# Rotary attention: both masks added by TensorE, GpSimd left with the head products, VectorE with plain maxima

## Chip, cores and metric

The kernel runs on one core of a Trainium2 chip. The metric is the device time of one execution in microseconds (us), lower is better. It is a chain of eight layers over 16 sequences of 512 tokens with 128 features, taken in pairs of sequences. The change touches one layer only, the third attention (rotary, causal, softmax).

## What is computed

The layer in question, cut to what matters. `x` is (16, 512, 128), there are 16 heads of 8 features. `_rope` with `d_param` = 128 multiplies each row by a table (the halves are never swapped, since `mid` is larger than the head).

```python
q = _rope(proj(Wq, bq), e)
k = _rope(proj(Wk, bk), e)
v = proj(Wv, bv)
att = jnp.einsum('bhqd,bhkd->bhqk', q, k) / scale
causal = jnp.tril(jnp.ones((t, t), dtype=bool))
att = jnp.where(causal[None, None], att, -jnp.inf)
att = jax.nn.softmax(att, axis=-1)
y = jnp.einsum('bhqk,bhkd->bhqd', att, v)
```

## The kernel before, in words

The program has three parts (`PARTS`), each a loop over the eight pairs of sequences, with an expert stage between the first and the second. The rotary attention is the first layer of the second part, so it runs eight times. Each loop body is written engine by engine; engines wait for one another by semaphores only, and each works through its own list in order.

**Quartets and steps.** The 16 heads of a sequence are four quartets, so a pair has eight (`QUARTETS`), numbered c. The four heads of a quartet lie in the four groups of 32 partitions. Work on a quartet is cut into six steps u. A step takes two heads and one set of tiles: the query tiles 3, 2, or 1 and 0 (`TILES_OF`), or the key tiles 0, 1, or 2 and 3 (`KEYS_OF`). So a step is 512, 384, or 256+128 columns wide for each of its two heads, and each width occurs in two steps.

**Two kinds of scores.** `scores(c, u)` makes row scores (queries on partitions), of which only the maximum of each row is wanted. `scores_t(c, u)` makes transposed scores (keys on partitions), of which the exponent is taken and which then weigh the values. The maxima are turned (`turn_max`) and added to the queries (`shift`), so that the transposed scores come out shifted. TensorE's list, for c from -2 to 8 and u from 0 to 5, is

```python
scores_t(c, u)
scores(c + 2, u)
```

with `values` (u = 0, 1, 4), `turn_max(c + 1)` (u = 1) and `spread_sums(c - 1)` (u = 3) behind them. All eight quartets thus pass in ten and a half rounds: two with row scores alone (c = -2, -1), six with both kinds (c = 0 to 5), two with transposed scores alone (c = 6, 7) and a rest. The two heads of `scores_t(c, u)` are `2 * (1 - u % 2) + e`, those of `scores(c + 2, u)` are `2 * (u % 2) + e`: the other two row groups of the array.

**Buffers.** Both kinds write three double banks of PSUM (`twin[n % 3]`) in turn (`SLOTS`). So `scores_t(c, u)` waits for the maxima of step u-2 (signal `l2_max`), and `scores(c + 2, u)` for the exponents of `scores_t(c, u - 1)` (`l2_exp`).

**Masks.** VectorE's `maxima` (line 792) is one `tensor_tensor_reduce` for each head and tile: it adds `mask_row` (zeros, then a triangle of -1e30) and takes the negated maximum, by a custom instruction and a read of its accumulator. The exponents are not masked; GpSimd's `mask` (lines 597 and 601) sets the blocks on the diagonal to zero with `affine_select` afterwards and raises `l2_masked`, for which `values` waits.

**Other work beside it.** A previous pair's last layer (attention over heads) is spread over this stage: GpSimd's `product` (line 651, 16 of them, two before the masks and 14 among them in `l2_masks`) and VectorE's `take` (lines 1364 and 1367), at fixed steps (`TAKE_STEP`). A product waits for the take two before it (`f_read`), a take for its product (`f_pool`). GpSimd's list in `l2_masks` is the masks of steps 0 and 1, a product, the masks of steps 2 to 5, a product, and so on for seven quartets.

**Names and lines.** TensorE: `scores` 1761, `scores_t` 1779, `values` 1802 (in `weigh`), `turn_max` 1848, `spread_sums` 1861, each of which a profile shows by its line; every fp32 matmul appears as two instructions in it. ScalarE: exponents 1435, `take_values` 1445, `invert` 1454 and 1456. VectorE: `divide` 808, `shift` 816.

Of the kernel before, what the change touches and what calls it, by code (L numbers as in the profile page):

```python
# [54 lines left out]
def program(nc, dram, x_in, out, sorted_x, sorted_y, kept_x, routes, returns, starts):  # L55
    with ExitStack() as ctx:
# [268 lines left out]
        for first, last in PARTS:  # L325
# [214 lines left out]
            with nc.Fori(0, SEQS // 2 if first < LAYERS else 1) as pair:  # L540
                sg = Signals()
                with nc.Block(no_gpsimd_drain=True) as block:
# [44 lines left out]
                    def _(pool):  # L587
                        def mask(tag, c, u):
# [4 lines left out]
                            p = at_pt[tag][n % len(at_pt[tag])]  # L593
                            pool.wait_ge(sg[tag + "_exp"], n + 1)
                            if u < 4:
                                p = p[:, :, 0:P]
                                pool.affine_select(p, p, [[0, 2], [1, P]], ALU.is_ge, 0.0, base=0,  # L597
                                                   channel_multiplier=-1).then_inc(sg[tag + "_masked"], 1)
                            else:
                                p = p.rearrange("p e (b k) -> p e b k", b=2)[:, :, :, 0:P]  # L600
                                pool.affine_select(p, p, [[0, 2], [0, 2], [1, P]], ALU.is_ge, 0.0, base=0,
                                                   channel_multiplier=-1).then_inc(sg[tag + "_masked"], 1)

                        def l1_masks():
# [22 lines left out]
                            for c in range(-2, QUARTETS + 1):  # L627
                                split(c + 1)
                                for u in range(STEPS_OF):
                                    mask("l1", c, u)  # L630
                                    if 0 <= c < QUARTETS and u % 3 == 1:
                                        send_rows(pool, sg, (2 * QUARTETS + 2 * c + u // 3,))
# [50 lines left out]
                        for layer in range(first, min(last, LAYERS)):  # L683
# [30 lines left out]
                            if layer == L2_ATTENTION:  # L714
# [3 lines left out]
                                l2_masks()  # L718
# [13 lines left out]
                    def _(dve):  # L732
# [43 lines left out]
                        def twin_attention(tag, beside):  # L776


                            def maxima(c, u):
# [5 lines left out]
                                for e in range(2):  # L785
                                    j = 2 * (u % 2) + e
                                    at = 0
                                    for i in TILES_OF[u // 2]:
                                        w = P * (i + 1)
                                        into = at_nmax[c % 4][:, i, j:j + 1] if tag == "l1" else at_shift[c % 2][  # L790
                                            :, i, j, DH:DH + 1]
                                        last = dve.tensor_tensor_reduce(  # L792
                                            s[:, e, at:at + w], s[:, e, at:at + w], W["mask_row"][:, T - w:T], -1.0, 3e38,
                                            ALU.add, ALU.min, into)
                                        at += w
                                last.then_inc(sg[tag + "_max"], 1)
# [903 lines left out]
                    def _(pe):  # L1700
# [23 lines left out]
                        def twin_attention(tag, row_sets, of_value, beside):  # L1724
# [16 lines left out]
                            def scores(c, u):  # L1741
# [801 lines left out]
```

## Time and profile before

| | us |
|---|---|
| median of 3 runs | 6046.7 (6040.18 to 6059.04) |
| profiled execution, first to last instruction (its span) | 6032.4 |
| PE busy / DVE busy / ACT busy / POOL busy | 4713.6 / 3697.0 / 1851.2 / 2161.3 |

The profiled execution shows its span; its own time is that and what lies around it, and the median of the runs is 14.3 us above the span. PE is TensorE's matmuls, PEld its weight loads, DVE VectorE, ACT ScalarE, POOL GpSimd. PE's busy time is to be read with care: matmuls overlap and their ends are modelled, so starts say more than durations. PEclk is the granted clock as a share of 2.4 GHz; it takes the values 1.0 and 0.5 (1.2 GHz), and anything between is a mean over a stretch.

The rotary attention of a pair is found by its first row scores and by the first instruction of the projection that follows it: 3595.5 and 3733.2 us for the third pair, and 136 to 140 us for each of the eight.

### The profile page before, as it was taken

The page shows a single profiled execution, that of the slowest core. Times are in us where ns is not written, and L with a number is a line of the kernel's source. Part 1 is how long each engine was busy: PE and PEld are TensorE (multiplying, and loading weights), DVE is VectorE, ACT ScalarE, POOL GpSimd, SP SyncE. Part 2 cuts the span into 40 slices and gives each one's busy share as a digit, 9 for nine tenths or more (in the row PEclk, how much of TensorE's full clock was granted, in tenths as well). Part 3 has the DMA queues.
Part 4 walks back from the last instruction along what each step waited for, and adds up shares of the span by engine and source line. Part 5 has one row for each costly group of instructions (what it writes and reads, how often), then busy time and mean ns, then how long its engine had stood idle before and what let it go on. Part 6 is the DMA issues. An engine that isn't in the chain of part 4 may idle for free. (4 is left out here: it accounts for less than half of the span.)

```text
span 6032.4 us, 97232 instructions
## 1 busy us (share of the span) xinstructions
PE 4713.6 (78%) x37160; PEld 2735.5 (45%) x37160; DVE 3697.0 (61%) x11081; ACT 1851.2 (31%) x2829; POOL 2161.3 (36%) x2704
## 2 busy tenths in 40 slices
PE   5979797979797979595877868778687786877772
PEld 3444445444444444363443544535435444354442
DVE  3646464646464646364768567686686766857765
ACT  2333343334333334242323224132331322412320
POOL 1323232323232222444525236153361443614525
PEclk9989898989898989797888888888888888888886
DMA  4000000000000000372000000000000000000000
GB/s 146 6 18 6 18 6 18 6 18 6 18 6 18 6 18 6 112 232 74 4 15 13 8 20 4 15 14 6 18 6 12 18 5 17 8 9 20 3 15 5
DMA packets 141914, 146.71 MB, mean 24 GB/s; under 512 B 31256, under 2 KB 126042, under 8 KB 141042
## 3 DMA queue, kind: packets, MB, share of 16 engines
q1 hardware_dynamic: 114274, 93.48, 5.3%
q0 software_dynamic: 18432, 37.79, 2.2%
q10 hardware_dynamic: 8736, 8.91, 0.5%
q8 instruction: 326, 5.34, 0.4%
q14 instruction: 146, 1.20, 0.1%
HBM read 69.64 MB, written 62.59 MB: 22 GB/s over the span
## 5 line engine op out<-in xcount | busy, mean ns | idle before, releaser
L792 DVE CUSTOM_DVE_ANT_0 twin<-twin,w_mask_row 128x512 f32<-128x512 f32 (+3 forms) x2048 | 951.0, 521 | 329.7 <-PE twin L1761 328.3
L1761 PE MATMUL twin<-arena 32*128 32x128 f32 (+3 forms) x4096 | 799.4, 517 | 39.6 <-DMA arena<-hres 16.8
L1779 PE MATMUL twin<-arena 32*128 32x128 f32 (+3 forms) x4096 | 784.2, 499 | 35.3 <-DVE arena L792 33.9
L1707 PE MATMUL twin<-w_ident_b 128*128 128x512 bf16 x1536 | 454.9, 450 | 383.7 <-DVE mv L752 157.9
L1435 ACT ACTIVATE arena<-twin 128x768 f32<-128x768 f32 (+1 forms) x544 | 479.3, 881 | 691.6 <-PE twin L1790 387.5
L1779 PEld LDWEIGHTS twin<-arena 32*128 32x128 f32 x4096 | 342.8, 195 | 471.7 <-issue 283.3
L695 POOL TENSOR_SCALAR ve<-mv 128x4 f32<-128x4 f32 x128 | 27.7, 216 | 1467.8 <-DVE mv L752 1467.2
L321 POOL DMA_INDIRECT got<-sorted_y,back x288 | 281.1, 976 | 539.6 <-ACT ring L1641 289.0
L1707 PEld LDWEIGHTS twin<-w_ident_b 128*128 128x128 bf16 x1536 | 157.7, 112 | 651.5 <-DVE mv L752 180.6
L313 POOL DMA_INDIRECT sorted_x<-got,w_mo_first_slots x288 | 282.4, 981 | 467.5 <-DVE ring L866 302.2
L1761 PEld LDWEIGHTS twin<-arena 32*128 32x128 f32 x4096 | 353.6, 204 | 196.8 <-issue 109.2
L1802 PE MATMUL twin<-arena 128*32 128x128 f32 (+3 forms) x2944 | 305.8, 459 | 18.6 <-POOL arena L597 18.6
L792 DVE DVE_READ_ACCUMULATOR2_ANT arena<- 128x1 f32 x2048 | 292.4, 143 | 0.0
L597 POOL TENSOR_SCALAR_AFFINE_SELECT arena<-arena 128x256 f32<-128x256 f32 x352 | 143.0, 409 | 342.7 <-ACT arena L1435 342.5
L1435 ACT ACTIVATE ring<-twin 128x768 f32<-128x768 f32 (+1 forms) x224 | 194.0, 878 | 198.6 <-PE twin L1779 197.6
L701 POOL TENSOR_TENSOR rs<-ve,minus_half 128x4 f32<-128x4 f32 x208 | 223.6, 1075 | 17.3
L2180 PE MATMUL twin<-w_l3f_we,arena 128*128 128x128 f32 x1152 | 191.1, 320 | 47.7 <-DVE arena L1115 47.7
L651 POOL TENSOR_TENSOR w_mo_wgu<-w_mo_wgu,w_l_cs_feat 128x2048 f32<-128x2048 f32 x36 | 197.3, 5483 | 54.5 <-DVE w_mo_wgu L1364 27.7
L1802 PE MATMUL twin<-ring,arena 128*32 128x384 f32 (+3 forms) x1152 | 155.7, 497 | 64.1 <-POOL ring L597 57.5
L651 POOL TENSOR_TENSOR w_mo_wgu<-w_mo_wgu 128x2048 f32<-128x2048 f32 x36 | 200.3, 5568 | 13.5 <-DVE w_l_wo L1367 13.5
L2180 PEld LDWEIGHTS twin<-w_l3f_we,arena 128*128 128x128 f32 x1152 | 163.9, 221 | 88.9 <-DVE arena L1115 63.6
L1364 DVE TENSOR_REDUCE w_mo_wgu<-w_mo_wgu 128x128 f32<-128x1024 f32 x144 | 174.6, 1217 | 22.6 <-POOL w_mo_wgu L651 22.6
(440 smaller groups left out, 10008.1 us busy)
## 6 DMA issues: line engine op xcount, KB each, us to landing
sorted_y<-arena SPq DMA_DIRECT2D x96, 256.0 KB, 2.8
sorted_x<-zeros ACTq DMA_DIRECT2D x2, 4096.0 KB, 19.9
a<-sorted_x SPq DMA_DIRECT2D x64, 128.0 KB
b<-sorted_x SPq DMA_DIRECT2D x64, 128.0 KB, 2.5
hres<-sorted_x SPq DMA_DIRECT2D x64, 128.0 KB
sorted_x<-got,w_mo_first_slots POOLq DMA_INDIRECT x288
got<-sorted_y,back POOLq DMA_INDIRECT x288
x_out<-w_l_w SPq DMA_DIRECT2D x18, 256.0 KB, 2.3
```

The costliest lines, as they stand in the source:

```text
L313: pool.indirect_dma_start(sorted_x[r % GROUPS], bass.IndirectOffsetOnAxis(ap=slot_of[:, q, n:n + 1], axis=0), normed[q][:, r // GROUPS], N ...
L321: pool.indirect_dma_start(got[q][:, n], None, sorted_y, bass.IndirectOffsetOnAxis(ap=back[:, q, n:n + 1].bitcast(U32), axis=0)).then_inc(s ...
L651: pool.tensor_tensor(pr, left.broadcast_to(shape), right.broadcast_to(shape), ALU.mult).then_inc(sg["f_pool"], 1)
L701: pool.tensor_tensor(RS[q][:], VE[q][:], minus_half[:], ALU.pow).then_inc(sg["rstd_ready"], 1)
L792: last = dve.tensor_tensor_reduce(s[:, e, at:at + w], s[:, e, at:at + w], W["mask_row"][:, T - w:T], -1.0, 3e38, ALU.add, ALU.min, into)
L1364: i = dve.tensor_reduce(ht_sc[q][:, t, heads], ht_pr[m % 2].rearrange("p (h g d) -> p h g d", h=H, g=H)[:, heads], AX, ALU.add)
L1435: act.activation(at_pt[tag][n % len(at_pt[tag])][:, :, 0:w], twin[SLOT["scores_t", c, u] % 3][:, :, 0:w], ACT.Exp, scale=1.0 if tag == "l1 ...
L1707: pe.matmul(into, ident_b, ident_b.unsqueeze(1).broadcast_to([P, NT, P]), start=True, stop=True, skip_group_check=True)
L1761: last = pe.matmul(s[:, e, at:at + w], queries[r, P * i:P * (i + 1)], keys[r, 0:w], start=(at == 0), stop=True, skip_group_check=True)
L1779: last = pe.matmul(s[:, e, at:at + w], keys[r, P * m:P * (m + 1)], queries[r, P * m:T], start=(at == 0), stop=(tag == "l2"), skip_group_ch ...
L1802: last = pe.matmul(bank[into][rows_of(j), P * m:T], weights(m, j), at_pt[tag][n % len(at_pt[tag])][:, j % 2, at:at + w], start=(m == 0), s ...
L2180: i = pe.matmul(pb3(q, 3)[:, t], mo_fb[q][:, (e - 1) % 2, t * P:(t + 1) * P], weights[:, (e - 1) * P:e * P], start=(e == 1 and t == 0), st ...
```

## The change

In the rotary attention (tag `l2`) only:

- `scores` adds, behind the score matmuls of each step, one bf16 matmul for each of the two heads: identity times the triangle of `mask_row`, onto the diagonal blocks (128 columns, or 256 in the steps with two tiles). VectorE's `maxima` becomes one plain `tensor_reduce` over both heads for each tile.
- `scores_t` adds the same with `mask_tb` on its diagonal blocks, so that the exponents come out masked. GpSimd's masks go, and `values` waits for `l2_exp` instead of `l2_masked`.
- GpSimd's list is then the 14 products one behind another.

```diff
-                        def l2_masks():
-                            for c in range(QUARTETS):
-                                for u in range(STEPS_OF):
-                                    mask("l2", c, u)
-                                    if u == 1 and c < HEAD_QUARTETS:
-                                        product(2 + 2 * c)
-                                if c < HEAD_QUARTETS:
-                                    product(3 + 2 * c)
+                        def head_products():
+                            for m in range(2, 4 * NT):
+                                product(m)
...
+                                j = 2 * (u % 2)
+                                if tag == "l2":
                                     at = 0
                                     for i in TILES_OF[u // 2]:
                                         w = P * (i + 1)
-                                        into = at_nmax[c % 4][:, i, j:j + 1] if tag == "l1" else at_shift[c % 2][
-                                            :, i, j, DH:DH + 1]
+                                        last = dve.tensor_reduce(at_shift[c % 2][:, i, j:j + 2, DH], s[:, :, at:at + w], AX,
+                                                                 ALU.max, negate=True)
+                                        at += w
+                                    last.then_inc(sg["l2_max"], 1)
+                                    return
...
                                     for e in range(2):
                                         r = rows_of(2 * (u % 2) + e)
                                         last = pe.matmul(s[:, e, at:at + w], queries[r, P * i:P * (i + 1)], keys[r, 0:w],
-                                                         start=(at == 0), stop=True, skip_group_check=True)
+                                                         start=(at == 0), stop=(tag == "l1"), skip_group_check=True)
                                     at += w
+                                if tag == "l2":
+                                    diagonal = slice(P * TILES_OF[u // 2][0], P * TILES_OF[u // 2][0] + P * len(TILES_OF[u // 2]))
+                                    masks = W["mask_row"][:, T - P:T].unsqueeze(1).broadcast_to([P, len(TILES_OF[u // 2]), P])
+                                    for e in range(2):
+                                        last = pe.matmul(s[:, e, diagonal], ident_b, masks, start=False, stop=True,
+                                                         skip_group_check=True)
                                 last.then_inc(sg[tag + "_scores"], 1)
...
+                                if tag == "l2":
+                                    for e in range(2):
+                                        blocks = s[:, e].rearrange("p (b k) -> p b k", b=2)[:, 0:len(KEYS_OF[u // 2]), 0:P]
+                                        masks = W["mask_tb"].unsqueeze(1).broadcast_to([P, len(KEYS_OF[u // 2]), P])
+                                        last = pe.matmul(blocks, ident_b, masks, start=False, stop=True, skip_group_check=True)
...
-                                pe.wait_ge(sg[tag + "_masked"], STEPS_OF * c + 2 * b + 2)
+                                pe.wait_ge(sg["l1_masked" if tag == "l1" else "l2_exp"], STEPS_OF * c + 2 * b + 2)
```

TensorE's list in a round with both kinds, steps 1 and 2, before (1779 transposed scores, 1761 row scores, 1848 `turn_max`, 1802 `values`):

```order
L1779 MATMUL twin<-arena 128x512 x2
L1761 MATMUL twin<-arena 128x512 x2
L1848 MATMUL twin<-w_ident,arena 128x128 x4
L1802 MATMUL twin<-arena 32x256 x4
L1802 MATMUL twin<-arena 32x128 x4
L1779 MATMUL twin<-arena 128x384 x2
L1761 MATMUL twin<-arena 128x384 x2
```

and the same steps now (1787, 1763, 1861 and 1815 are those lines moved; 1794 and 1770 are the masks):

```order
L1787 MATMUL twin<-arena 128x512 x2
L1794 MATMUL twin<-w_mask_tb,w_ident_b 128x128 x2
L1763 MATMUL twin<-arena 128x512 x2
L1770 MATMUL twin<-w_mask_row,w_ident_b 128x128 x2
L1861 MATMUL twin<-w_ident,arena 128x128 x4
L1815 MATMUL twin<-arena 32x256 x4
L1815 MATMUL twin<-arena 32x128 x4
L1787 MATMUL twin<-arena 128x384 x2
L1794 MATMUL twin<-w_mask_tb,w_ident_b 128x128 x2
L1763 MATMUL twin<-arena 128x384 x2
L1770 MATMUL twin<-w_mask_row,w_ident_b 128x128 x2
```

Where transposed and row scores stood next to each other, a pair of masks now stands between them and another behind them.

GpSimd's list from the first products on, before (651 products, 597 and 601 masks):

```order
L651 TENSOR_TENSOR w_mo_wgu<-w_l_wo,w_l_cs_feat 128x2048 x2
L597 AFFINE_SELECT arena<-arena 128x2x128 x2
L651 TENSOR_TENSOR w_mo_wgu<-w_l_wo,w_l_cs_feat 128x2048
L597 AFFINE_SELECT ring<-ring 128x2x128 x2
L601 AFFINE_SELECT ring<-ring 128x4x128
L601 AFFINE_SELECT arena<-arena 128x4x128
L651 TENSOR_TENSOR w_mo_wgu<-w_l_wo,w_l_cs_feat 128x2048
```

and all of it now:

```order
L651 TENSOR_TENSOR w_mo_wgu<-w_l_wo,w_l_cs_feat 128x2048 x4
L651 TENSOR_TENSOR w_mo_wgu<-absorbed_q,w_mo_wgu 128x2048 x4
L651 TENSOR_TENSOR w_mo_wgu<-w_mo_wgu,w_l_cs_feat 128x2048 x4
L651 TENSOR_TENSOR w_mo_wgu<-w_mo_wgu 128x2048 x4
```

The 16 products keep their order; the 48 masks of a pair are gone from between them.

## Rows read from the trace of the kernel before

**Rows 1.** The page: its span.
```profile
span 6032.4 us, 97232 instructions
```

**Rows 2.** Windows of one pair: stretch, length, busy PE, PEld, DVE, ACT, POOL, clock
```profile
3595.50:3611.70 16.20, 14.07 (x70) 7.90 (x70) 14.91 (x52) 0.00 (x0) 7.71 (x2) 0.58 0.13 25
3611.70:3703.00 91.30, 75.31 (x600) 31.32 (x600) 86.67 (x251) 42.82 (x54) 71.60 (x48) 0.89 0.03 7
3703.00:3733.20 30.20, 23.47 (x154) 8.79 (x150) 11.81 (x14) 14.23 (x20) 22.27 (x15) 0.76 0.00 1
```

**Rows 3.** Windows, one round of the first pair, same columns.
```profile
2847.50:2858.20 10.70, 10.54 (x108) 4.81 (x100) 9.15 (x35) 5.60 (x7) 10.70 (x7) 1.00 0.13 25
```

**Rows 4.** Timeline of PE in one round: start us, duration, instruction, count
```profile
3649.40 1.06 PE L1802 MATMUL twin<-ring,arena 128*32 128x512 f32 x8
3650.40 0.48 PE L1779 MATMUL twin<-arena 32*128 32x256 f32 x2
...
3651.18 1.07 PE L1779 MATMUL twin<-arena 32*128 32x512 f32 x4
3652.32 1.13 PE L1761 MATMUL twin<-arena 32*128 32x512 f32 x4
3653.38 0.52 PE L1802 MATMUL twin<-arena 128*32 128x384 f32 x2
...
3654.16 0.70 PE L1779 MATMUL twin<-arena 32*128 32x512 f32 x2
3654.18 0.70 PE L1761 MATMUL twin<-arena 32*128 32x512 f32 x2
...
3654.71 0.59 PE L1761 MATMUL twin<-arena 32*128 32x512 f32 x2
3655.23 0.66 PE L1848 MATMUL twin<-w_ident,arena 128*128 128x128 f32 x4
3655.82 0.41 PE L1802 MATMUL twin<-ring,arena 128*32 128x256 f32 x2
...
3656.61 0.59 PE L1779 MATMUL twin<-arena 32*128 32x384 f32 x2
...
3657.04 0.49 PE L1779 MATMUL twin<-arena 32*128 32x384 f32 x2
...
3661.18 1.10 PE L1861 MATMUL twin<-hres,w_sel_sum 128*128 128x512 f32 x2 [1.50 <-issue]
3662.20 0.48 PE L1779 MATMUL twin<-arena 32*128 32x256 f32 x2
```

**Rows 5.** Timeline of PE in another layer: a 512-column bf16 identity times mask.
```profile
3105.57 0.63 PE L2247 MATMUL twin<-w_mask_tb,w_ident_b 128*128 128x512 bf16 x1
3106.00 0.63 PE L2255 MATMUL twin<-arena 128*128 128x128 f32 x2
```

**Rows 6.** Groups by line, 3645.1 to 3660.4: count | busy, mean ns | idle before
```profile
L792 DVE CUSTOM_DVE_ANT_0 twin<-twin,w_mask_row 128x384 f32<-128x384 f32 (+3 forms) x16 | 7.4, 518 | 0.6 <-PE twin L1761 0.6
...
L1364 DVE TENSOR_REDUCE w_mo_wgu<-w_mo_wgu 128x128 f32<-128x1024 f32 x4 | 4.9, 1216 | 0.0
```

**Rows 7.** Timeline of DVE, two maxima by their widths.
```profile
3654.90 0.69 DVE L792 CUSTOM_DVE_ANT_0 twin<-twin,w_mask_row 128x512 f32<-128x512 f32 x1
...
3649.60 0.43 DVE L792 CUSTOM_DVE_ANT_0 twin<-twin,w_mask_row 128x256 f32<-128x256 f32 x1 [0.61 <-PE twin L1761]
```

**Rows 8.** Groups by line, 2600 to 5900 us: slowest products, matmuls that weigh values.
```profile
L651 POOL TENSOR_TENSOR w_mo_wgu<-w_mo_wgu 128x2048 f32<-128x2048 f32 x32 | 178.5, 5579 | 13.5 <-DVE w_l_wo L1367 13.5
...
L1802 PE MATMUL twin<-ring,arena 128*32 128x384 f32 (+3 forms) x1152 | 155.7, 497 | 64.1 <-POOL ring L597 57.5 <-POOL ring L601 6.1
...
L1802 PE MATMUL twin<-arena 128*32 128x256 f32 (+3 forms) x896 | 128.6, 500 | 18.6 <-POOL arena L597 18.6
```

**Rows 9.** Windows, a dense stretch of the same pair, columns as in rows 2.
```profile
3622.00:3640.00 18.00, 17.75 (x154) 7.21 (x146) 16.63 (x59) 9.64 (x13) 16.05 (x14) 1.00 0.08 16
```

**Rows 10.** Timeline at the pair's end: ScalarE takes the last values.
```profile
3729.46 0.60 ACT L1445 ACTIVATE arena<-twin 128x512 f32<-128x512 f32 x1 [1.69 <-PE twin L1802]
```

More of the change, by code:

```diff
@@ L587, in _, with mask @@
                     def _(pool):
-                        def mask(tag, c, u):
+                        def mask(c, u):
                             if not 0 <= c < QUARTETS:
@@ L592, in mask @@
                             n = STEPS_OF * c + u
[L593 to L594 removed]
+                            p = at_pt["l1"][n % len(at_pt["l1"])]
+                            pool.wait_ge(sg["l1_exp"], n + 1)
                             if u < 4:
@@ L629, in l1_masks @@
                                 for u in range(STEPS_OF):
-                                    mask("l1", c, u)
+                                    mask(c, u)
                                     if 0 <= c < QUARTETS and u % 3 == 1:
@@ L784, in maxima @@
                                 s = twin[SLOT["scores", c, u] % 3]
-                                for e in range(2):
-                                    j = 2 * (u % 2) + e
+                                j = 2 * (u % 2)
+                                if tag == "l2":
                                     at = 0
@@ L789, in maxima @@
                                         w = P * (i + 1)
-                                        into = at_nmax[c % 4][:, i, j:j + 1] if tag == "l1" else at_shift[c % 2][
-                                            :, i, j, DH:DH + 1]
+                                        last = dve.tensor_reduce(at_shift[c % 2][:, i, j:j + 2, DH], s[:, :, at:at + w], AX,
[4 more added lines that the diff above has]
+                                for e in range(2):
+                                    at = 0
+                                    for i in TILES_OF[u // 2]:
+                                        w = P * (i + 1)
                                         last = dve.tensor_tensor_reduce(
                                             s[:, e, at:at + w], s[:, e, at:at + w], W["mask_row"][:, T - w:T], -1.0, 3e38,
-                                            ALU.add, ALU.min, into)
+                                            ALU.add, ALU.min, at_nmax[c % 4][:, i, j + e:j + e + 1])
                                         at += w
-                                last.then_inc(sg[tag + "_max"], 1)
+                                last.then_inc(sg["l1_max"], 1)
                             def divide(c):
@@ L1779, in scores_t @@
                                         last = pe.matmul(s[:, e, at:at + w], keys[r, P * m:P * (m + 1)], queries[r, P * m:T],
-                                                         start=(at == 0), stop=(tag == "l2"), skip_group_check=True)
+                                                         start=(at == 0), stop=False, skip_group_check=True)
                                     at += w
+                                if tag == "l2":
+                                    for e in range(2):
+                                        blocks = s[:, e].rearrange("p (b k) -> p b k", b=2)[:, 0:len(KEYS_OF[u // 2]), 0:P]
+                                        masks = W["mask_tb"].unsqueeze(1).broadcast_to([P, len(KEYS_OF[u // 2]), P])
+                                        last = pe.matmul(blocks, ident_b, masks, start=False, stop=True, skip_group_check=True)
                                 if tag == "l1":
```

6 lines of the change are left out of this document (3 added, 3 removed).

## Prediction

> **What bounds the kernel now.** The page gives the span, 6032.4 us [rows 1]; the median of the runs is 14.3 us above it, and I carry that difference along. The change touches one stage that runs eight times, so the windows come next, cut where its kinds of round change [rows 2]. A pair's rotary attention is 16.2 + 91.3 + 30.2 = 137.7 us, eight of them some 1100 us of the span. In the middle stretch (six rounds with both kinds of scores, 15.2 us each) DVE is busy 86.67 of 91.3 us, 95%, and POOL 71.6. PE's 75.3 is 82%, at a granted clock of 0.89. So DVE bounds the middle, with the maxima and the takes in its list. In the tail DVE is busy 11.8 of 30.2 us: there PE waits for masks that stand in POOL's list behind products of up to 5.58 us [rows 8]. The groups by line show that wait: matmuls of `values` found PE idle for 64.1 + 18.6 = 82.7 us over the eight pairs, and nearly all of it ended by a mask [rows 8].
>
> The margin of PE matters most, and the busy column hides it. It has to be read from starts in PE's timeline [rows 4]. The transposed scores of a 512 step alone start at 3651.18, the row scores of the next at 3652.32 and what follows at 3653.38: 1.14 and 1.06 us apart, each for two heads. At 3654.16 and 3654.18 both kinds start together, on the four different row groups, and the next instruction starts at 3655.23: 1.07 us for **four** heads. The second kind costs nothing where it stands next to the first. That is what keeps PE below DVE. The round of the first pair at 2847.5, before the takes weigh on DVE, shows PE's floor: 10.54 busy of 10.70 us at clock 1.00 [rows 3].
>
> **PE in a round, now.** From starts [rows 4]: a 512 step costs 1.07 us; a 384 step twice the distance 3656.61 to 3657.04, 0.86; a 256+128 step 3650.40 to 3651.18, 0.78. Two of each are 5.42. `values` is 1.00 (3649.40 to 3650.40), 0.78 (3653.38 to 3654.16) and 0.79 (3655.82 to 3656.61), 2.57 together; `turn_max` 0.59; `spread_sums` 1.02 (3661.18 to 3662.20). With both kinds overlapping in five steps of six (step 0 is apart, +1.07) that makes 5.42 + 1.07 + 2.57 + 0.59 + 1.02 = 10.67, which is the 10.70 of [rows 3].
>
> **What the masks do to it.** A mask is an identity matmul over all 128 rows. PE takes its matmuls in order, so the masks of `scores_t` wait until its two row groups have streamed, and `scores` on the other two groups waits for the masks. None of the six steps can overlap any more: the two kinds cost 2 x 5.42 = 10.84. The masks themselves are 12 pairs in a round, eight of 128 and four of 256 columns. Streaming alone: 512 bf16 columns took 0.43 us at half clock (3105.57 to 3106.00) [rows 5], so 0.055 per 128 at full clock, 8 x 0.11 + 4 x 0.22 = 1.8 us. That is the low bound. For the high bound I take `turn_max`, whose four transposes cost 0.59 with both handovers, 0.15 each: 8 x 0.30 + 4 x 0.41 = 4.0. I take 3.0, since of the two rows the transposes are the nearer for the handovers and the bf16 row for the streaming. A round with both kinds is then 10.84 + 3.0 + 2.57 + 0.59 + 1.02 = **18.0 us of PE**, against 15.2 us that it takes today. PE becomes the bound.
>
> In the trace the full-array transpose starts 0.52 us after the last pass over 32 rows (3654.71 to 3655.23), as far as one pass lies behind the other (3654.18 to 3654.71) [rows 4]: the switch costs nothing extra there, and the sum has no term for it. The Trainium skill (TensorEngine Tiling (Array Packing), Tiling Modes) says that changing the tiling mode, not just the tile, drains the engine. By that rule each of a round's 24 switches would cost extra; the trace does not agree, by that 0.52, and it is among the rivals below.
>
> **DVE and POOL.** The maxima of a round are 16 custom instructions, 7.4 us busy [rows 6]. Width costs 0.26 us per 256 elements, on top of 0.17 (0.69 at 512, 0.43 at 256) [rows 7], and a 1024-wide reduce, from SBUF, takes 1.22 [rows 6], on the same line. Eight reduces of 1024, 768, 512, 256 (twice) are 5120 elements and eight fixed parts: 5.2 + 1.4 = 6.6, so 0.8 us less, and the accumulator reads go too. Taking both, DVE needs some 14.2 us where it had 15.2. That is below 18.0 and no longer on the path. Its reduces are done in time: PE needs the maxima of step u-2 for `scores_t(u)`, and at least 2 us of other PE work now lie between. The 48 selects removed from POOL are worth nothing in the middle (cover: PE's own 18 us); in the tail they end PE's waits. The 14 moved products wait only for takes. Two products take at most 11.2 us [rows 8] of an 18 us round, so they are early, and in the tail the last three end some 17 us after its start, inside PE's 27. No DMA moves, SP's list stays as it is, and ScalarE's exponents are the same. `values` now waits for the exponents alone, which are two or more steps old. The edit of `stop` in the earlier attention changes no instruction count; I cost it at nothing.
>
> **The sum for a pair.** Middle: six rounds of 18.0 = 108.0 against 91.3, +16.7. Start (16.2 us now): twelve row-score groups, 10.84, twelve pairs of masks, 3.0, and a `turn_max`, 0.59, are 14.4 at full clock. The mean clock there is 0.58, mostly the lower level of 1.2 GHz, after PE has waited for the rotated rows and with DVE setting its pace [rows 2]; it is 1.00 where PE is packed, 17.75 of 18 us [rows 9]. PE will now be packed from the start; I allow 6 us at half clock, costing 3: 17.4, +1.2. Bounds: 14.4 (-1.8) and all at half clock, 28.8 (+12.6). Tail (30.2 now): round 6 is 5.42 + 1.5 + 2.57 + 0.59 + 1.02 = 11.1, round 7 10.5, the last two `values` 1.6 and the chain from there to the end 3.8 (3729.46 to 3733.2) [rows 10]: 27.0, -3.2. Waits at handovers, 0.16 a round as in [rows 3]: +1.3. Together +16.0 a pair, x 8 = **+128 us**: 6046.7 + 128 = 6175.
>
> **Rivals.**
> - *DVE stays the bound, faster.* If the masks only queue between scores that go on overlapping, PE needs 10.7 + 3.0 = 13.7 a round, below DVE's 14.2. Then six rounds give -6, the start -2, and the tail loses its mask waits, -6: -14 a pair, 5935. It decides where PE's round falls below 14.2. For it: the handover to the transpose is free, and nothing in the trace shows a full-array matmul between two row groups that could overlap. Against it: in rows 4 no full-array instruction starts before the row groups have had their whole pass, and the masks stand between the kinds in every step. 0.12.
> - *Nothing to measure.* Masks at their low bound (16.8 a round) and a fast start and tail leave +3 a pair; it would need 1 us more of luck. With a partial overlap the sum crosses zero: 6047. 0.05.
> - *Drains.* If each switch waits for the pipeline to empty, its price is the 0.16 by which a 384 pass (0.59) outlasts the 0.43 to the pass behind it [rows 4]; 24 switches are 3.8 us a round, and over the eight quartets 31 a pair: +47, 6423. Against it: the 0.52 above. 0.07.
> - *The change isn't what it says.* PE's and POOL's lists show it is: masks between the kinds, products in one row. No chance is kept for it.
>
> **How the numbers follow.** The forecast has 0.76. Its own range: low, masks 1.8 (six rounds 100.8, +9.5), start -2.4, tail -4.2: +3 a pair, 6070. High, masks 4.0 (19.0 a round, +22.7), start +14.6, tail -1: +36, 6337. A measurement of this kernel can tell about 0.3%, 18 us, from no change. The faster rival lies outside the range and so does the drain; of the forecast's own spread the range keeps nearly all: 6075 to 6335. Faster 0.12, same 0.05, slower 0.76 + 0.07 = 0.83.
>
> **What would show it.** In the profile after: rounds in the middle of 17 to 19 us; PE's starts of 1763 always behind a mask, never within 0.02 us of 1787; a granted clock near 1.0 in the middle; DVE down from 95% to below 80% there; no wait of 1815 for POOL; about 108 us for the middle and 27 for the tail. Wrong it is if starts of 1763 still fall together with those of 1787's two heads, if a mask pair costs over 0.4 us, or if the half clock lasts through the start.

## The result: 7% slower, and the profile after

The changed kernel takes 6484.3 us, median of 4 runs (6468.4 to 6541.8); the kernel before, run beside it, 6043.4 (6028.9 to 6059.0). The ratio is 1.074, with a 95% interval of 1.070 to 1.078. The forecast was 6175, its range 6075 to 6335, so the sign and the bound are right, and the size is off by 309 us, outside the range. Medians and ratios here leave out executions in a slower state, of which there were two: 6604.0 us in the run with key masks alone, and 8213.6 us of the kernel before. In the changed kernel's lines `scores` is 1763, `scores_t` 1787, the row masks 1770, the key masks 1794, `values` 1815, `turn_max` 1861 and the maxima 785.

The span on the page of after; and, from the groups by line of 2600 to 6200 us, the two groups of `values`, with the idle time before them in the last column:
```profile
span 6479.0 us, 98384 instructions
```
```profile
L1815 PE MATMUL twin<-ring,arena 128*32 128x384 f32 (+3 forms) x1152 | 175.2, 552 | 0.2
...
L1815 PE MATMUL twin<-arena 128*32 128x256 f32 (+3 forms) x896 | 142.3, 544 | 0.0
```
`values` found PE idle for 82.7 us before [rows 8]; now it is 0.2 us. `values` no longer waits for POOL's masks. That part did what it was to do.

Windows over whole pairs, from the first row scores to the output projection. First the kernel after, its third, fifth and sixth pair and the sum of all eight; columns as in [rows 2]:
```profile
...
3701.20:3884.10 182.90, 177.88 (x1009) 73.71 (x1009) 109.21 (x123) 58.19 (x74) 78.33 (x16) 0.79 0.03 6
...
4580.80:4785.40 204.60, 199.63 (x1008) 80.55 (x1008) 109.37 (x123) 58.21 (x74) 78.29 (x16) 0.70 0.03 5
5034.70:5216.20 181.50, 176.50 (x1009) 73.42 (x1009) 109.15 (x123) 58.18 (x74) 78.30 (x16) 0.80 0.03 6
...
sum 1543.50, PE 1503.19 PEld 614.79 DVE 873.94 ACT 465.57 POOL 625.63; mean PE 187.90 PEld 76.85 DVE 109.24 ACT 58.20 POOL 78.20
```
The same for the kernel before, its third pair and the sum of all eight:
```profile
3595.50:3733.20 137.70, 112.85 (x816) 48.01 (x816) 113.40 (x315) 57.06 (x74) 101.58 (x64) 0.83 0.04 7
...
sum 1097.60, PE 903.09 PEld 384.36 DVE 908.68 ACT 456.82 POOL 807.65; mean PE 112.89 PEld 48.05 DVE 113.59 ACT 57.10 POOL 100.96
```
The stage grew by 1543.5 - 1097.6 = 445.9 us and the span by 446.6: all of the loss is here. PE is busy 97% of the stage, DVE 57%. And the pairs, which run the same instructions, differ by 23 us, with the granted clock: 0.70 in the slowest, 0.80 in the fastest. The clock is what has to be read next.

Windows of the slowest pair, round by round:
```profile
4580.80:4604.70 23.90, 23.87 (x94) 10.43 (x94) 15.46 (x18) 0.00 (x0) 11.53 (x3) 0.56 0.14 26
4604.70:4632.90 28.20, 28.20 (x103) 11.26 (x102) 8.23 (x11) 5.29 (x6) 5.17 (x2) 0.50 0.06 11
4632.90:4665.80 32.90, 32.90 (x129) 12.58 (x128) 10.38 (x12) 7.05 (x9) 4.49 (x1) 0.50 0.00 0
4665.80:4690.00 24.20, 24.20 (x128) 9.52 (x130) 14.47 (x17) 7.98 (x10) 8.99 (x2) 0.72 0.00 1
4690.00:4708.00 18.00, 18.00 (x128) 7.88 (x130) 13.62 (x17) 7.03 (x9) 9.96 (x2) 1.00 0.00 1
...
4743.90:4785.40 41.50, 36.55 (x187) 13.21 (x186) 19.47 (x19) 15.86 (x21) 16.29 (x3) 0.67 0.00 0
```
PE is busy without a gap from the start of the pair on, and still has the lower clock, 1.2 GHz, for the start and two rounds and a half. Then the clock rises to 2.4 GHz, and a round with the same 128 matmuls takes 18.00 us instead of 32.90. The mean falls again in the tail, to 0.67. The other seven pairs do the same over shorter stretches: their six rounds take 116 to 131 us, and in all eight the last three rounds are 18.0 us at 1.00. In the kernel before, the half clock of the third pair ended within the first round, and the second ran at 1.00:
```profile
3611.70:3623.70 12.00, 11.62 (x77) 5.26 (x77) 11.20 (x43) 4.39 (x5) 5.72 (x5) 0.72 0.13 24
3623.70:3635.60 11.90, 11.71 (x108) 5.04 (x106) 10.68 (x36) 6.90 (x10) 9.95 (x7) 1.00 0.11 20
```

The timeline of PE at 1.00 shows what a step has become:
```profile
2904.78 1.13 PE L1787 MATMUL twin<-arena 32*128 32x512 f32 x4
2905.84 0.28 PE L1794 MATMUL twin<-w_mask_tb,w_ident_b 128*128 128x128 bf16 x2
2906.06 1.13 PE L1763 MATMUL twin<-arena 32*128 32x512 f32 x4
2907.12 0.28 PE L1770 MATMUL twin<-w_mask_row,w_ident_b 128*128 128x128 bf16 x2
2907.33 0.85 PE L1815 MATMUL twin<-ring,arena 128*32 128x384 f32 x8
...
2910.45 0.28 PE L1770 MATMUL twin<-w_mask_row,w_ident_b 128*128 128x128 bf16 x2
2910.57 0.61 PE L1861 MATMUL twin<-w_ident,arena 128*128 128x128 f32 x4
```
Each kind has its own 1.06 us now, where both shared 1.07 before [rows 4], and a pair of masks costs 0.21 to 0.22 with both switches. Ahead of another full-array product, the transposes of `turn_max`, it costs 0.12 (2910.45 to 2910.57). So there are two losses: the order of the round, and the clock in which it runs.

### The profile page after: what moved, and what is told of

Same layout as the page of the kernel before. It is cut to its first block and busy times, and to the rows that moved or that the text cites. A ratio compares the mean times of both kernels' runs of the same rounds, so it can differ in the third digit from the quotient of the medians.

```text
span 6479.0 us, 98384 instructions
## 1 busy us (share of the span) xinstructions
PE 5309.6 (82%) x38696; PEld 2964.1 (46%) x38696; DVE 3666.7 (57%) x9545; ACT 1859.5 (29%) x2829; POOL 1976.2 (31%) x2320
## 5 line engine op out<-in xcount | busy, mean ns | idle before, releaser
L1763 PE MATMUL twin<-arena 32*128 32x512 f32 (+3 forms) x4096 | 877.0, 534 | 20.5 <-DMA arena<-hres 16.8
L1787 PE MATMUL twin<-arena 32*128 32x512 f32 (+3 forms) x4096 | 867.0, 525 | 1.3
L785 DVE TENSOR_REDUCE arena<-twin 128x2 f32<-128x1024 f32 (+3 forms) x512 | 409.8, 822 | 502.3 <-PE twin L1770 502.1
L794 DVE CUSTOM_DVE_ANT_0 twin<-twin,w_mask_row 128x512 f32<-128x512 f32 (+3 forms) x1024 | 478.6, 520 | 274.0 <-PE twin L1763 273.0
L1787 PEld LDWEIGHTS twin<-arena 32*128 32x128 f32 x4096 | 370.2, 207 | 453.8 <-issue 303.5
L1763 PEld LDWEIGHTS twin<-arena 32*128 32x128 f32 x4096 | 370.8, 210 | 178.4 <-issue 126.7
L1815 PE MATMUL twin<-arena 128*32 128x128 f32 (+3 forms) x2944 | 319.6, 472 | 0.0
L651 POOL TENSOR_TENSOR w_mo_wgu<-absorbed_q,w_mo_wgu 128x2048 f32<-128x2048 f32 x36 | 162.1, 4507 | 399.0 <-DVE w_mo_wgu L1366 399.0
L651 POOL TENSOR_TENSOR w_mo_wgu<-w_l_wo,w_l_cs_feat 128x2048 f32<-128x2048 f32 x36 | 160.7, 4477 | 229.8 <-DVE w_mo_wgu L1366 156.9
```

The costliest lines, as they stand in the source:

```text
L651: pool.tensor_tensor(pr, left.broadcast_to(shape), right.broadcast_to(shape), ALU.mult).then_inc(sg["f_pool"], 1)
L785: last = dve.tensor_reduce(at_shift[c % 2][:, i, j:j + 2, DH], s[:, :, at:at + w], AX, ALU.max, negate=True)
L794: last = dve.tensor_tensor_reduce(s[:, e, at:at + w], s[:, e, at:at + w], W["mask_row"][:, T - w:T], -1.0, 3e38, ALU.add, ALU.min, at_nmax ...
L1787: last = pe.matmul(s[:, e, at:at + w], keys[r, P * m:P * (m + 1)], queries[r, P * m:T], start=(at == 0), stop=False, skip_group_check=True)
L1815: last = pe.matmul(bank[into][rows_of(j), P * m:T], weights(m, j), at_pt[tag][n % len(at_pt[tag])][:, j % 2, at:at + w], start=(m == 0), s ...
```

## The experiments

Two theories stood against each other. A: the masks between the kinds end their overlap; this costs PE its margin, and PE's unmerged passes over 32 rows leave the clock at 1.2 GHz, however busy it is. B: the mask products themselves hold the clock down, or cost more than they show. The clock after a dense burst, the overlap and the masks are varied one at a time. Each ratio is to the kernel before, run on the same chip; before had medians of 6023 to 6040 us there.

**Only the key masks on PE.** DVE's masked maxima as before.
```diff
-for e in range(2):
-    last = pe.matmul(s[:, e, diagonal], ident_b, masks, start=False, stop=True,
-                     skip_group_check=True)
...
-last = dve.tensor_reduce(at_shift[c % 2][:, i, j:j + 2, DH], s[:, :, at:at + w], AX,
-                         ALU.max, negate=True)
+last = dve.tensor_tensor_reduce(
+    s[:, e, at:at + w], s[:, e, at:at + w], W["mask_row"][:, T - w:T], -1.0, 3e38,
+    ALU.add, ALU.min, into)
```


> The changed kernel with DVE's old masked maxima: only the masks of the transposed scores are on PE. They stand between the transposed group and the group of scores of the same step, so they break one of the two meetings. Theory A: with one break left PE's round at full clock is 15.5 to 16.5 us, the half clock lasts into the rounds but shorter than in the changed kernel: 6200 to 6400 us. Rival B (each mask costs the same, wherever it is): halfway, 6200 to 6320. Rival D (DVE's plain maxima are what cost time): under 6100 us.

6528.9 us (6504.9 to 6599.9), ratio 1.083 (1.077 to 1.089): no faster than with both masks (1.070 to 1.078), and outside what any of the three theories gave. Windows of one pair (its six rounds), then one round at each clock:
```profile
5075.20:5251.30 176.10, 176.07 (x658) 70.12 (x660) 84.43 (x239) 42.45 (x53) 52.85 (x11) 0.50 0.02 3
```
```profile
5100.00:5130.30 30.30, 30.30 (x118) 11.89 (x116) 11.59 (x36) 7.05 (x9) 4.47 (x1) 0.50 0.00 1
3783.00:3799.30 16.30, 16.30 (x115) 7.22 (x114) 14.62 (x41) 7.04 (x9) 9.51 (x3) 1.00 0.00 1
```
At full clock this round is 1.7 us shorter than 18.0, as a round should be that has no overlap either and six pairs of masks fewer (10.84 for the scores, 4.2 for the rest and some 1.4 for six pairs). The only meeting that overlapped before is the one between the two kinds of the same step: `scores(c + 2, u)` and the next `scores_t(c, u + 1)` have the same two row groups. So key masks alone end all of the overlap, not half of it, as the expectation had it. The run lost because it left the half clock late or never: in three pairs the six rounds took 176 us, with PE busy for 176.07 of 176.10 in the pair shown; in the other five they took 112 to 169. The Trainium skill (TensorE: Matmul & The Clock Gate, The HAM clock gate) says that activity releases the throttle and that a busy PE runs warm. By that rule these six rounds would have taken some 98 us, six times 16.3; the trace does not agree, and the measurement decides.

**The overlap reduced without any mask on PE.** The kernel before, with the transposed scores on the row groups of their neighbour.
```diff
-r = rows_of(2 * (1 - u % 2) + e)         # scores_t
+r = rows_of(2 * ((1 - u % 2) if tag == "l1" else u % 2) + e)
...
-n = STEPS_OF * c + 2 * b + 1 - j // 2    # weigh: the buffer of a head's exponents
+n = STEPS_OF * c + 2 * b + (1 - j // 2 if tag == "l1" else j // 2)
```


> The kernel before with one line's worth of difference: the transposed scores of a step use the same two row groups as its scores, so that the first of the two meetings of a step no longer runs side by side. No mask is on PE. It breaks the meeting that the run with key masks alone broke (6564 us there, with half clock for up to 176 us a pair). Theory A (loss of the overlap, not the mask products, keeps the clock down): PE's round at full clock is 14.5 to 15.2 us, half clock lasts into the rounds of most pairs, time 6200 to 6550 us. Rival B (the mask products keep it down): clock as before, round near 15, time 6030 to 6110 us.

6214.9 us (6186.4 to 6226.6), ratio 1.029 (1.024 to 1.034). One pair, start, six rounds and tail; then one round of another pair:
```profile
4051.30:4067.50 16.20, 14.09 (x70) 7.92 (x70) 14.95 (x52) 0.00 (x0) 7.67 (x2) 0.55 0.13 25
4067.50:4175.90 108.40, 101.69 (x582) 46.47 (x584) 83.12 (x239) 40.93 (x52) 67.06 (x43) 0.74 0.03 6
4175.90:4212.00 36.10, 26.73 (x173) 9.88 (x169) 21.40 (x26) 16.25 (x22) 26.62 (x20) 0.76 0.00 0
```
```profile
3676.80:3700.50 23.70, 23.70 (x107) 10.44 (x106) 11.50 (x36) 7.05 (x9) 11.66 (x8) 0.50 0.01 2
```
The six rounds grow from 86 to 108 us and their clock falls from 0.90 to 0.74, with no mask on PE; the round of the last line is packed and stays at 0.50. So less overlap is enough to lower the clock, which speaks for A.

Here the clock went in and out, and in the run before it stayed down much longer. The two do not lose the same: with this edit, the scores of a step and the transposed scores of the next lie on different row groups, and there they run side by side. The timeline shows it (1761 is `scores`, 1779 the next step's `scores_t`):
```profile
3676.81 0.64 PE L1761 MATMUL twin<-arena 32*128 32x256 f32 x2
3676.82 1.22 PE L1779 MATMUL twin<-arena 32*128 32x512 f32 x2
```
The overlap has moved and shrunk, not gone: a packed round at half clock takes 23.7 us here and 30.3 with the key masks, of which their six pairs are some 2.4 (0.32 us each at 128 columns, 0.54 at 256). What is still open is why the key masks alone kept the clock down longer than both masks did.

**A dense burst ahead of the start, or ahead of the rounds.** The changed kernel, and 18 bf16 products of 512 columns from its own `keep_busy`, once before the row scores of a pair, once before the first round with both kinds.
```diff
 pe.wait_ge(sg["l2_v"], 2)
+keep_busy(bank[6], *[(None, 0)] * 3)     # ahead of the start
```
```diff
 for c in range(-2, QUARTETS + 1):
+    if (tag, c) == ("l2", 0):            # ahead of the rounds
+        keep_busy(bank[6], *[(None, 0)] * 3)
```


> The changed kernel with 18 plain bf16 products of 512 columns on PE ahead of each pair's rotary stage, which the kernel uses elsewhere to keep PE busy. Theory A, first form (the clock needs dense full-array work to rise, and once up stays up in the masked mix): the burst costs 4 to 8 us a pair, the start and the first rounds then run at 18 us and under instead of 26 us and over, 20 to 50 us a pair less: 6150 to 6350 us. Second form (the masked mix itself draws the clock down at the start, whatever came before it): half clock in the start and the first rounds again, time 6480 to 6560 us.

> The changed kernel with the burst of 18 dense bf16 products of 512 columns moved from ahead of the start to ahead of the first round with both kinds. In the run with the burst ahead of the start the start ran at full clock in 15.6 us and the clock fell again in the first round. If the masked, unmerged rounds can hold the full clock once they have it (they do late in every pair), all rounds are 18.0 us: middle 108 us against 116 to 139, burst 5 to 8 us, time 6310 to 6400 us. If the clock falls in the first rounds whatever came before, 6450 to 6560 us.

The first: 6405.7 us, ratio 1.064 (1.058 to 1.070), between the two forms that I had written down. The start gained, 15.6 us in all eight pairs; the rounds did not, 115 to 153 us. One pair, start and rounds, and the beginning of the rounds of another:
```profile
3243.80:3259.40 15.60, 14.64 (x93) 6.86 (x92) 13.44 (x16) 0.00 (x0) 5.86 (x3) 1.00 0.14 25
3259.40:3412.60 153.20, 153.17 (x730) 61.36 (x730) 76.46 (x89) 42.39 (x53) 53.30 (x11) 0.65 0.02 4
```
```profile
2826.60:2854.00 27.40, 27.36 (x98) 11.02 (x98) 9.99 (x13) 5.29 (x6) 8.08 (x2) 0.50 0.09 16
```
The second: 6288.9 us, ratio 1.044 (1.038 to 1.050), some 190 us below the changed kernel for one burst a pair, and a little below the range written down. One pair, start with burst, rounds, tail:
```profile
4494.80:4524.00 29.20, 29.18 (x110) 12.61 (x110) 16.57 (x20) 0.00 (x0) 12.21 (x3) 0.59 0.14 26
4524.00:4629.40 105.40, 105.40 (x731) 46.33 (x730) 73.06 (x84) 42.36 (x53) 49.84 (x10) 1.00 0.01 2
4629.40:4661.80 32.40, 27.31 (x188) 10.53 (x186) 19.60 (x19) 15.74 (x21) 16.33 (x3) 0.89 0.00 1
```
The instructions of these rounds are those of the changed kernel. There they took 116 to 139 us; lifted once, they hold 1.00 to the end and take 105.4 in all eight pairs. So the mask products do not hold the clock down (against B), and at full clock PE's rounds cost what the sum said. The row scores of the start leave PE at 1.2 GHz, and unmerged rounds climb out of it late. The level at which the rounds begin does not settle it alone: behind the burst ahead of the start they began at 1.00 too, and the clock fell in the first round. Behind a burst directly ahead, the same first round, without `values` in both runs, held 1.00 and took 15.5 us. What in the start makes that difference is open.

**The overlap restored.** The changed kernel, both kinds next to each other and both groups of masks behind them.
```diff
 scores_t(c, u)
 scores(c + 2, u)
+if tag == "l2":
+    mask_keys(c, u)                      # was inside scores_t
+    mask_rows(c + 2, u)                  # was inside scores
```


> The changed kernel, with the two score groups of a step again next to each other and both groups of mask products behind them. Theory A (what the change lost is the overlap of the two kinds of scores, and while it is lost the granted clock stays near 0.5): the groups share PE again, so a round at full clock costs PE 5.7 (scores) + 2.2 to 3.0 (masks) + 2.57 + 0.59 + 1.02 = 12 to 13 us, DVE's 12.5 or so becomes the bound, the clock rises after the start of a pair as in the kernel before, and the time is 5930 to 6080 us. Rival B (the masks' full-array products themselves hold the clock down or cost far more than 0.22 to 0.33 us a pair): the half clock stays for 50 to 95 us a pair as in the changed kernel, time over 6250 us.

6078.5 us (6048.1 to 6114.6), ratio 1.009 (1.005 to 1.013): some 400 us below the changed kernel with the same instructions, only reordered. PE in one step and its masks (in this kernel 1794 is `scores_t`, 1763 `scores`, 1819 the key masks, 1777 the row masks), then one whole pair, then one round at full clock:
```profile
2861.04 0.49 PE L1794 MATMUL twin<-arena 32*128 32x384 f32 x2
2861.06 0.49 PE L1763 MATMUL twin<-arena 32*128 32x384 f32 x2
2861.48 0.29 PE L1819 MATMUL twin<-w_mask_tb,w_ident_b 128*128 128x128 bf16 x2
2861.60 0.28 PE L1777 MATMUL twin<-w_mask_row,w_ident_b 128*128 128x128 bf16 x2
2861.80 0.59 PE L1794 MATMUL twin<-arena 32*128 32x384 f32 x2
```
```profile
3601.70:3625.60 23.90, 23.90 (x92) 10.34 (x92) 15.43 (x18) 0.00 (x0) 11.41 (x3) 0.56 0.14 25
3625.60:3709.80 84.20, 83.67 (x731) 39.48 (x730) 73.89 (x87) 41.50 (x53) 48.34 (x11) 0.98 0.02 5
3709.80:3751.30 41.50, 36.56 (x188) 13.19 (x186) 19.46 (x19) 16.61 (x22) 18.65 (x4) 0.67 0.00 0
```
```profile
2866.47:2880.36 13.89, 13.89 (x127) 6.54 (x126) 13.66 (x17) 7.29 (x11) 9.30 (x3) 1.00 0.00 1
```
The kinds start together again (2861.04 and 2861.06), the half clock ends within the first round, in this pair and in the others, and the six rounds take 84.2 us (84 to 89 over the eight pairs), where they took 86 before (86 to 89). PE is still the bound of them, 99% busy: the expectation that DVE would be it was off by a little (DVE is at 88%, and at 13.66 of 13.89 us in the full round). What is left of the loss is in the start (24 to 26 us, 16 before) and in the tail (31 to 43, before 33 to 36), where only one kind exists and the masks still part the groups.

**Parts of it.** Three smaller runs. Row masks on PE alone, key masks on POOL; then the same with the row masks issued only where an overlap ends anyway; then plain maxima with no row mask at all (that part is left out).
```diff
 scores(c + 2, u)
+if tag == "l2":                          # second run: row masks placed
+    if c + 2 < QUARTETS:
+        unmasked.append((c + 2, u))
+    if u % 2 if c < 0 else u not in (2, 5):
+        while unmasked:
+            mask_rows(*unmasked.pop(0))
```


> The kernel before, with row masks alone on PE, behind the group of scores, and plain maxima on DVE; the masks of the transposed scores stay products of Pool. A row mask now stands behind each second group, so half of the meetings of the two kinds are left. Theory A: PE's round is 1 to 1.5 us longer than before and stays at or under 14.4 us, DVE is 0.8 to 1.1 us shorter, time 5990 to 6100 us. Rival B (masks hold the clock): half clock well into the pair's rounds, time over 6150 us. Rival C (Pool's products were the bound of the tail): tails unchanged at 33 to 36 us, since Pool's work is unchanged.

> The kernel before with row masks on PE and plain maxima on DVE as in the run with row masks alone (6073 us), but the row masks are issued only where the groups' overlap ends anyway: in the start behind every second group, in the rounds ahead of the value, turn and sum products, never between the scores of one step and the transposed scores of the next. Key masks stay on Pool. Theory A: the start falls from 24 to 16 us a pair, the rounds lose the broken meetings: 5980 to 6020 us, at or under the kernel before. Rival (the maxima that come a step later delay the slots or the shift): 6040 us and more.

> The kernel before with plain maxima of two heads on DVE in the rotary stage and no mask of the row scores at all (that part of the computation is left out: the maxima are taken over unmasked scores, which changes the shift of the exponents). DVE's gain alone, with nothing added to PE: if DVE bounds the full-clock rounds of before, 0.8 to 1.1 us a round less, 5970 to 6000 us; if PE at half clock or Pool bound them, 6020 to 6035 us, no difference.

6073.3 us (ratio 1.010, 1.006 to 1.013), 6086.9 (1.011, 1.009 to 1.014) and 5989.9 (0.994, 0.992 to 0.997). The last is the value of the plain maxima on DVE: 35 us when nothing is paid for it. The first pays 83 us by the medians, over 90 by the ratios, for the row masks that make it possible. They leave the overlap of the rounds as it is, since each stands where the groups are the same anyway. The start pays for them, and for the overlap that they end between its groups; before it was 16.2 us and PE was not full:
```profile
3974.20:3998.00 23.80, 23.80 (x92) 10.38 (x92) 15.41 (x18) 0.00 (x0) 7.69 (x2) 0.56 0.14 26
```
The second was a miss. Its starts fell to between 16 and 20 us, but its rounds rose to 94. Waits of some six rounds in it (790 is the maxima, 1780 the row masks, 1800 `scores_t`):
```profile
DVE arena L790 <- PE twin L1780: 19.2, 13, 3.3
...
PEld twin L1800 <- DVE arena L790: 16.0, 18, 1.7
```
DVE, 95% busy in these rounds before, gets two maxima at once and then waits 19.2 us for masks, and the transposed scores wait for it. This fits the rival named there; I did not test it further.

**Masks behind two groups in the start and tail, and bursts.** First the reordered kernel with masks behind every second group where only one kind exists; then with 12 burst products ahead of the rounds; then bursts of 6 products ahead of the quartets of the tail as well, and the tail's masks directly behind their groups.
```diff
 if tag == "l2":
-    mask_keys(c, u)
-    mask_rows(c + 2, u)
+    alone = c < 0 or c + 2 >= QUARTETS   # third run: alone = c < 0
+    for v in (u,) if not alone else (u - 1, u) if u % 2 else ():
+        mask_keys(c, v)
+        mask_rows(c + 2, v)
```
```diff
 s = slot("scores_t", c, u)
+if tag == "l2" and u == 0 and c >= QUARTETS - 2:   # third run
+    keep_busy(s[:, 0], (None, 0))
```


> The run with adjacent groups (6078 us), and in the start of a pair and in its last two quartets, where only one kind of scores is issued, masks wait for two groups and go behind both, so that these two run side by side as well. Theory A: the start falls from 24 to 26 us to 16 to 18 us and the tail from 41 to 34 to 38 us, 10 to 14 us a pair: 5950 to 6010 us, which would beat the kernel before. Rival (the half clock in the start depends on what came before it, not on the overlap): start stays at 24, time 6060 to 6090 us.

> The run with masks behind two groups (6078 us), and a burst of 12 dense bf16 products of 512 columns ahead of the first round of each pair. Theory A (the clock of the first rounds is what PE got just before, and then holds): the first round falls from 16.5 to 19.6 us to 13.9, the burst costs 2.6 us at full clock and 5.2 at half: between 3 us a pair less and 2 more, 6055 to 6095 us; every round at clock 1.00. Rival: the clock falls again in the first round: 6100 to 6130 us.

> The run with masks behind two groups and a burst ahead of the rounds (6052 us), but in the last two quartets each group's masks stand directly behind it again, and 6 dense bf16 products of 512 columns go ahead of the first transposed group of each of these two quartets. Theory A (what the masked tail costs is the half clock it falls to: 31 to 32 us where it ran at 0.89 to 0.94, 41 to 43 at 0.63 to 0.67): the tail keeps the full clock, 32 to 34 us with the bursts against 35 to 38, 2 to 5 us a pair less: 6010 to 6040 us, level with the kernel before. Rival (the lost overlap in the tail costs more than the clock gives): tails of 37 us and over, 6055 us and more.

The first took 6078.1 us (ratio 1.009), no better than without: a miss. Its profile has the expected start, one pair:
```profile
3984.70:4000.90 16.20, 14.01 (x92) 7.39 (x92) 13.33 (x16) 0.00 (x0) 9.08 (x3) 0.91 0.14 26
4000.90:4090.50 89.60, 89.08 (x731) 42.16 (x730) 75.58 (x89) 41.48 (x53) 50.73 (x11) 0.90 0.03 7
4090.50:4127.30 36.80, 30.14 (x188) 11.84 (x187) 19.54 (x19) 15.79 (x22) 18.76 (x4) 0.77 0.00 0
```
Eight such pairs are 67 us shorter than in the run without (1143.7 against 1210.5), yet the spans differ by 37 and the medians by nothing. The other 30 us lie outside the stage, 7 ahead of the first pair and 22 between the pairs; and the profiled execution of the run without lay 33 us above its own median. The stretch ahead of the first pair, which no run changes, ended between 2778 and 2826 us in the profiles of this document, so spans by themselves do not show differences of this size. Why the medians are level stays open.

The second took 6052.1 us (1.005, 1.003 to 1.008), with all six rounds at 1.00. The third took **6012.1 us** (5997.0 to 6024.2), against 6039.5 for the kernel before, a ratio of 0.994 (0.992 to 0.997). It beats the changed kernel by some 7%, and the kernel before by some 0.5%, which is small, though the interval leaves out 1. One pair, start, rounds, tail:
```profile
3974.80:3995.50 20.70, 18.55 (x104) 9.12 (x104) 16.15 (x20) 0.00 (x0) 12.19 (x3) 0.84 0.14 26
3995.50:4080.00 84.50, 83.97 (x737) 39.66 (x736) 73.91 (x87) 42.25 (x53) 48.95 (x10) 1.00 0.03 6
4080.00:4109.60 29.60, 25.80 (x193) 10.36 (x192) 18.25 (x17) 15.71 (x21) 17.39 (x4) 1.00 0.00 1
```
The tail, with masks between its groups, takes 29.6 us at 1.00; with the same order of scores and masks it took 41.5 at 0.67 in the pair shown of the reordered kernel, and 32.0 at 0.89 in another.

**The burst in the kernel before.** The same 12 products ahead of its rounds.

> The kernel before with a burst of 12 dense bf16 products of 512 columns ahead of the first round of each pair. Its rounds have gaps on PE and its clock falls in and out of 1.00 (mean 0.90 in the middle). Theory A: the first round is lifted (12 to 15 us at 0.5 to 0.7 before), the later falls stay, since they follow PE's idle stretches and not what came ahead of the rounds: between 0 and 5 us a pair slower, 6025 to 6070 us. Rival (one lift holds here too): middle 86 to 80 us, 5980 to 6010 us.

6035.8 us, ratio 1.001 (0.999 to 1.004), as theory A had it: in a kernel that DVE bounds and that reaches the full clock early, a burst ahead of the rounds buys nothing. So that burst by itself does not explain the third run's gain. The bursts in the tail were not tried in the kernel before, whose tail ran at 0.76 in the third pair; whether they would gain as much there is open.

## Why the prediction was wrong

*What bounds it* was right: PE is the bound after the change, DVE is at 14.18 us of a full 18.0 us round where I had 14.2 (12.4 as the mean of six rounds, since the first ones have fewer takes), POOL's products wait only for takes, and `values` waits for no mask.

*The round at full clock* was right in each term, to 0.2 us. The sum said 10.84 for the unmerged scores, 3.0 for the masks and 4.18 for the rest, 18.0; by the starts, the trace has 11.04, 2.82 and 4.12, 17.98 from the `scores_t` at 2904.78 to the one at 2922.76. That the 3.0 came so near is partly luck: it was a choice between 1.8 and 4.0. In the reordered kernel the round is 13.89 us, 3.2 above the 10.70 of [rows 3], but only 2.2 of that are masks, which stand behind one another there; the other 1.0 is scores, most of it in step 3, where the kinds start 0.86 us apart (2876.00 and 2876.86). The drain rival is refuted in its size by the mask rows: it had 0.32 us for the two switches of a pair, and a pair with both costs 0.21, of which 0.12 remain where another full-array product follows. So the switches cost about 0.09 us a pair. The prediction's "costs nothing extra" was read from a switch into the full array alone; the cost shows at the switch out of it.

*The step that failed* is this one: "PE will now be packed from the start; I allow 6 us at half clock, costing 3". It read [rows 9], a packed stretch at 1.00, as if being packed gave the clock. In that stretch both kinds overlapped and the clock was already up. Now PE is packed as well, and stays at 1.2 GHz. The size of it, from the rows: at full clock the parts of a pair were measured as 15.6 (the start behind a burst), 105.4 (the rounds behind a burst) and 28.3 (the tail of the last run, 29.6 less its burst of 1.3), 149.3 together. The sum without its allowance had 150.7 (14.4 + 108.0 + 27.0 + 1.3). A pair of the changed kernel takes 1543.5 / 8 = 192.9, so some 44 us a pair go to the half clock, where the sum had 3. Together 149.3 + 43.6 - 137.2 = +55.7 a pair, which is the 445.9 / 8 measured, against +16.0. All of the error is in this term. The bound of "all at half clock, 28.8" was there, but for the start alone; the same bound on the rounds (32.9) would have widened the range to hold the result. The list of what would make the prediction wrong ended with the half clock; it should have had a chance.

*A cut was misplaced.* I took 3703.0 for the end of the six rounds, but the first transposed group of quartet 6 starts at 3697.7:
```profile
3611.70:3697.70 86.00, 72.73 (x588) 30.81 (x588) 81.37 (x239) 41.14 (x53) 66.30 (x43) 0.90 0.04 7
3697.70:3733.20 35.50, 26.05 (x163) 9.30 (x162) 17.11 (x26) 15.92 (x22) 27.57 (x20) 0.76 0.00 0
```
A round took 14.3 us, not 15.2, and the tail 35.5, not 30.2. The pair's total is the same, so the sum is not touched, but the terms were: +22 and -8.5 instead of +16.7 and -3.2. DVE's share of the middle was 95% either way.

*The tail* at 27.0 was right for the full clock (29.6 with a burst of 1.3 us in it) and wrong for the clock that it gets, 41.5 at 0.67.

*The rival "DVE stays the bound"* named the condition on which this hangs: 13.7 us for a round where the overlap survives. The reordered kernel has it at 13.9. With masks behind two groups in the start and the clock kept up by bursts it is 0.5% faster than before.

## What to carry to other kernels

Small matmuls on different row groups share the array only while nothing that takes all rows stands between them. Put identity products, transposes and masks behind the whole set of groups, not behind each. And when a change takes such overlap away, price the new order at both clocks: a PE that is 100% busy with passes over 32 rows is not sure to get the full one, and a short dense burst directly ahead of such a stretch tells in one run whether the clock is what costs. One stage earlier it did not: the start had the clock, and the rounds lost it again.

## What the runs showed of the hardware

- The same stream of matmuls ran at either clock: six rounds in 105.4 us at 1.00 behind a burst, 139.2 us at a mean of 0.73 in the slowest pair without it. With key masks alone it was 176.1 us at 0.50 with PE busy 176.07.
- What came ahead matters, but not for ever: behind a burst the start held 1.00 for all its 15.6 us, and the first round fell to 0.50 with PE busy 27.36 of 27.40 us. Behind a burst directly ahead of them the rounds held 1.00 to their end, in all eight pairs.
- A pair of 128-column masks costs 0.12 us ahead of another full-array product and 0.21 to 0.22 ahead of passes over 32 rows or into 32 columns (2907.12 to 2907.33): leaving the full array costs about 0.09 us.
- Masks of the two kinds behind one another cost less than apart: 0.12 us from the first pair to the second and 0.20 to what follows (2861.48, 2861.60, 2861.80), where a pair alone took 0.21 to 0.22.
